# A two-layer transformer kernel whose written-out order of steps (an order table of letters) is replaced by another one

## What is computed

```python
x = x + L0_attn(layernorm(x))   # 16 heads of 8, causal softmax over 1024 tokens, W_qkv, W_out
x = x + L0_ffn(layernorm(x))    # ifft(fft(x) @ w), a real 128x128 matrix here, + bias
x = x + L1_attn(layernorm(x))   # the same attention, per-head 8x8 Wq, Wk, Wv, then Wu, bu
x = x + L1_ffn(layernorm(x))    # 8 experts of 256, the best 2 of a softmax gate, gelu
```

## Time and profile before

| | before |
|---|---|
| median of 3 runs (lowest to highest) | 1220.77 us (1218.82 to 1221.8) |
| the profiled execution: time / span of its trace | 1220.89 / 1219.2 us |
| busy in the span: TensorE, VectorE, ScalarE, GpSimd | 1132.4, 901.7, 770.1, 401.4 us |
| first shift copied at / last shift copied at | 78.9 / 923.4 us |
| last exponential of the last group ends | 958.4 us |
| the experts' steady chain begins | 986.9 us |

### The profile page before, as it was taken

One profiled execution on the slowest core, in us unless ns is written; L12 is line 12 of the kernel. 1 busy time (PEld: TensorE's weight loads), 2 busy tenths in 40 slices (PEclk: granted clock), 3 DMA queues, 4 the chain that ended last, 5 costly groups with the idle time before them and its releaser, 6 DMA issues. The chain is left out here.

```text
span 1219.2 us, 26837 instructions
## 1 busy us (share of the span) xinstructions
PE 1132.4 (93%) x9927; PEld 542.5 (44%) x9927; DVE 901.7 (74%) x1461; ACT 770.1 (63%) x1397; POOL 401.4 (33%) x667
## 2 busy tenths in 40 slices
PE   3479999999999999999999999999999799999997
PEld 2224343444344344433444344433342357777776
DVE  4698889998998999898899998898892253223223
ACT  1327678777888778787777787777777542322322
POOL 3143452555226462555356452142252000000000
PEclk9669999999999999899999999999998989999999
DMA  3230420112111011002111210011100000000000
GB/s 108 94 115 28 123 79 29 28 28 73 53 29 35 28 54 53 28 29 66 53 37 34 79 29 28 27 34 47 30 3 2 1 1 1 17 0 17 0 18 18
DMA packets 35336, 47.35 MB, mean 39 GB/s; under 512 B 8848, under 2 KB 15120, under 8 KB 35216
## 3 DMA queue, kind: packets, MB, share of 16 engines
...
q10 hardware_dynamic: 576, 0.15, 0.1%
...
## 5 line engine op out<-in xcount | busy, mean ns | idle before, releaser
L748 ACT ACTIVATE probs<-psum 128x512 f32<-128x512 f32 x1152 | 614.3, 604 | 199.8 <-PE psum L634 197.6
L930 DVE TENSOR_REDUCE block_max<-psum 128x8 f32<-128x1024 f32 x576 | 672.3, 1218 | 70.4 <-PE psum L602 67.0
L634 PE MATMUL psum<-q_rows,k_rows 50*128 50x512 bf16 (+3 forms) x1536 | 325.1, 330 | 14.4 <-ACT probs L748 10.9
L657 PE MATMUL psum<-probs,vg 128*32 128x512 f32 (+3 forms) x3072 | 329.0, 504 | 7.4 <-POOL probs L857 4.4
L857 POOL TENSOR_SCALAR_AFFINE_SELECT probs<-probs 128x512 f32<-128x512 f32 (+1 forms) x320 | 173.9, 547 | 448.0 <-ACT probs L748 444.4
L602 PE MATMUL psum<-k_rows,q_rows 48*128 48x128 bf16 (+2 forms) x2560 | 261.4, 266 | 27.8 <-DMA k_rows<-k_split 17.7
L602 PEld LDWEIGHTS psum<-k_rows,q_rows 48*128 48x128 bf16 x2560 | 114.7, 95 | 180.6 <-DVE block_max L930 74.9
L634 PEld LDWEIGHTS psum<-q_rows,k_rows 50*128 50x128 bf16 x1536 | 105.1, 94 | 166.0 <-ACT probs L748 124.0
L1162 DVE SCALAR_TENSOR_TENSOR x<-psum,probs,x 128x128 f32 x256 | 69.1, 343 | 144.4 <-PE psum L1080 144.0
L1102 ACT ACTIVATE probs<-psum 128x1024 f32<-128x1024 f32 x64 | 65.5, 1024 | 151.5 <-PE psum L1067 151.5
L1080 PEld LDWEIGHTS psum<-w_out,probs 128*128 128x128 f32 x1024 | 119.2, 192 | 14.8 <-issue 12.9
(11 more groups left out here) (107 smaller groups left out, 617.4 us busy)
## 6 DMA issues: line engine op xcount, KB each, us to landing
k_rows<-k_split SPq DMA_DIRECT2D x384, 32.0 KB
...
q_rows<-shift_t SPq DMA_DIRECT2D x64, 8.0 KB
```

The costliest lines, as they stand in the source:

```text
L634: done = nc.tensor.matmul(m.psum[:, bank, col:col + w], m.k_rows[rows_of(e, True), buf, pair, kb * P:(kb + 1) * P], m.q_rows[rows_of(e, Tr ...
L657: done = nc.tensor.matmul(m.psum[32 * hh:32 * hh + 32, OUT_BANK, q0 % BANK:q0 % BANK + w], m.vg[:, n % 2, kb, hh, :], m.probs[:, (n * len( ...
L748: nc.scalar.activation(out, m.psum[rows, UNIT_AT[number % UNIT_DEPTH], 0:columns], function, **more).then_inc(bank_read, 1)
L930: nc.vector.tensor_reduce(out, blocks, axis=AX.X, op=ALU.max).then_inc(ring_read, 1)
```

## The change

31 of the 33 lines of `LINES` are written anew, all but the first and the last; nothing else is touched. Every stream keeps its steps and their order, so the same instructions run, on the same engines, with the same sizes and numbers of buffers. The banks of the ring are given out in the new order. Two of the lines:

```diff
@@ -112,37 +112,37 @@
 LINES = (
     "xxxxxxxxxxxxxxxxxxxxwwwxxxxxxrrxxxrxxrxxrxxrxxrxxxxxxxrrrrrrrrrrrrrHrrr",
...
-    "uuvuruvruuvcruuurvOuruuvruxuruvuruvcxHuuvruruvuruuuvruruuuvruruuurvuruuwr",
...
-    "uxuvruvuruxruvcruuurvuOuruuvruuvruuuvcuuuvHuvuuuvuuuuvuuuuvuuu",
...
+    "uvruvuruuruvcruuxOuruuvruuruvvuruuvcruuruvruuvruruuvuruuxxuuuvuuHruvuuwrvvrxvc",
...
+    "uvruvuruuvcruuruvOuruuruvuvruuruvcuruuvruruuvuruuvruruuuvuuuuHvuuu",
     "uuvuvuuvcuuuvOuuuvvuuuvcuuuvuuuuvuuuuvuuuuvuuuuvuuuxxvvvcOxxxxxxxxxxxxxxxxxxx",
 )
```

More of the change, by code:

```diff
@@ L120 @@
[L120 to L137, removed]
@@ L145 @@
-    "uxuvruvuruxruvcruuurvuOuruuvruuvruuuvcuuuvHuvuuuvuuuuvuuuuvuuu",
+    "uuuruxxxxuruuruvuuuvvuuuvcuuuvuuxuvururuxuvruruxruuvruuxrurxuuvururuwxrxvxHvvxrrcxxO",
+    "uurxrxuuruuruvxxururuuuruvuvxrurxuuvcuruuxxxxxvuvuuurruvuuuuvuuuxuvuuruwxrxrxrvxxHvxxrrvxxcxr",
+    "uurxOxuruuruuvxxruruuuruuvrxuvxuruurvcuuruxvruuvruruuvruuuruvuHuuurruvuruw",
+    "uvruvuruuvcruuruvOuruuruvuvruuruvcuruuvruruuvuruuvruruuuvururuuvHuuuwrrvvrvc",
+    "uruuruuOuuruvruruuvuvruurxvcruuxrvuruuruuvruruuuvuruxxuuuvuuHruvuuuwrvrvx",
@@ new lines @@
+    "uruuvcruuruOuuruvxruruuvvuruuruvcxxruuvruruxxuvruruuuvruuxxuuuvuuHruvuuuwrvrvx",
+    "uruuvcruuruOuuruvrxuruuvuruvruuxxruvcruuurvruuvruuxxruruuvuruxHuuvruruxruuvrxuw",
+    "uxrxuruvuuvruruuvcruxxOuruxrxuurvuruxxrxxuurvvurxuurxuvcuruuvxuHuvruruuvuruuvruuruvuwr",
+    "uuvruuruvuruuvcruuruvOuruuvvruuxruvcruxruruuvuruuvHuuvruruuvuruuruvuruuwr",
+    "uuvruuruvuruuvcruuruvOuruuvvruuuvcruruuvruruuvuruuvHuuuvruruuuruvuruw",
+    "uvruvuruuruvcruuuOuruvuruuvruvruuuvcruruuvruruuvruuxxuuuvuHuurvuuuvruwrvvx",
@@ new lines @@
+    "uruuvcruuuruOuruuvrurxuuvurvuruuxvcrxruuvruuxxruvruruuvruuxxuuuvuuHruvuuuwrvrvx",
+    "uruuvcruuruOuuruvrxuruuvuruvruuxxruvcruuurvruuvruuxxruruuvuruxHuuvruruxruuvrxuw",
+    "uxrxuruvuuvruruuvcruxxOuruxrxuurvuruxxrxxuurvvurxuurxuvcuruuvxuHuvruruxuvruruxuvruruuvuwr",
+    "uruuvurvuruuvcruuruvOuruuvvruuuvcruruuvruuxxuuuvuHuruvuuuvruruuvuruuwr",
+    "uuvruvxuruuruvcruuuOuruvurxuurvuvruuuvcxrxruuvruruuvruuxxruvuHuuvruruuvuruuwr",
+    "uuvruvuruuruvcruuuOuruvuruurvuvruuuvcruruuvruruuvruuxxuuuvuuHvuruuvrxuwvrv",
@@ new lines @@
+    "uruuruuruuvcruuurvuOxuruuvruvxuruxruvcruuurvuruxxruuvruruuvuruxHuuvruruuvuwr",
+    "uxruurvuvurxuuruvcruuOuurxxruuvruurxxvruuvruuvcruxxruruuvuruxxxxxxHxvruruxuvruruxuvruruuvuwr",
+    "uruuvurvuruuvcruuruvOuruuvvruuuvcruruuvruuxxuuuvuHuruvuuuvruuruvuruuwr",
+    "uuvruvxuruuruvcruuuOuruvurxuurvuvruuuvcxrxruuvruruuvruuxxruvuHuuvruruuvuruuwr",
+    "uuvruvuruuruvcruuuOuruvuruurvuvruuuvcruruuvruruuvruuxxuuuvuuHvuruuvrxuwvrv",
+    "uruuruuruuvcruuurvuOxuruuvruvxuruxruvcruuurvuruxxruuvruruuvuruxHuuvruruuvuwr",
@@ new lines @@
+    "uxruurvuvurxuuruvcruuOuurxxruuvruurxxvruuvruuvcruxxruruuvuruxxxxxxHxvruruxuvruruxuvruruuvuwr",
+    "uruuvurvuruuvcruuruvOuruuvvruuuvcruruuvruuxxuuuvuHuruvuuuvruuruvuruuwr",
+    "uuvruvxuruuruvcruuuOuruvurxuurvuvruuuvcxrxruuvruruuvruuxruvuHuuvruruuvuruxruw",
+    "uvruvuruuruvcruuxOuruuvruuruvvuruuvcruuruvruuvruruuvuruuxxuuuvuuHruvuuwrvvrxvc",
+    "uuruOuururuuuvrxuruuvuruvruuxxruvcruuurvruuvruuxruruuvuruuvHuuurruvuruw",
+    "uvruvuruuvcruuruvOuruuruvuvruurxvcruuxrvuruuruvururuuvuruuxxuuuvuuHruvuuwrvvrxvc",
```

12 lines of the change are left out of this document (1 added, 11 removed).

## The result

| | before | after |
|---|---|---|
| median (lowest to highest), us | 1219.8 (1217.97 to 1221.8, 4 runs) | 1206.8 (1204.89 to 1209.52, 4 runs) |
| ratio, 95% interval | | 0.9898 [0.9882, 0.9913] |
| profiled execution / its span | 1220.89 / 1219.2 | 1209.52 / 1207.8 |

The account below looks back on a forecast made before the run. Neither engine alone was taken as bound: VectorE 90% full, TensorE nearly as full, time lost where long TensorE steps precede needed scores. 1220.9 - 6.2 (end) - 11.6 (places) + 2.1 + 1.8 = 1207.0 us; range 1193 to 1223, forecast's own 1200 to 1214.

Parts of the forecast that it names:

- The end: Behind the last shift: 3 units and one values step instead of 15 and 4 before group 31's first unit, 6.2 us less.
- The places: First to last shift: fewer scores, out steps and shifts right behind values steps, so VectorE idles 11.6 us less.
- +2.1: Ahead of the last shift: 12 units and 3 values steps moved there cost TensorE 0 to 4.2 us; middle taken.
- +1.8: Seven more shifts closely followed by their own group, waiting for the shift's DMAs: 0 to 3.6 us, middle taken.
- the dear place: Score directly behind a unit and a values step: its maximum found VectorE idle 0.248 us, against 0.037 at other scores.
- Norm steps: GpSimd's norm halves closer to their transpositions, ten first halves at the tight distance: 0 to 4 us, taken as 0.
- 1 (only the end): Nothing won in the middle, VectorE's idle time only moves; the end's gain stays: 1215 to 1219 us, chance 0.19.
- 6 (VectorE alone): VectorE the only bound, an order could close all its holes: 1128 us, chance 0.01.
- Of 2: More goes: the middle gives 22 us, nothing given back, perhaps one clock dip gone: 1193 us; below 1200, chance 0.11.
- the dip near 500 us: Granted clock at half around 500 us, VectorE idling 2.4 of 10 us instead of 1.0; it may go.
- Of 4: Slower through more stretches at half clock, about 1.4 us of VectorE each, some twelve more needed; chance 0.03.

Follow-up runs that it names:

- experiment 5: Kernel before with only the end of the order made as in the changed kernel (3 units and one values step behind the last shift): 1218.21 us, ratio 0.9990.
- experiment 3: Kernel before with 139 places 'unit, values, score' written as 'values, unit, score': 1228.29 us, ratio to before 1.0074.
- experiment 11: Kernel before with 36 values steps of the second half moved to later places only, by at most six letters: 1221.75 us, ratio 1.0011.
- experiment 6: Kernel before for its first 1229 letters (to about the shift of group 15), the changed kernel's order behind: 1201.65 us, ratio 0.9856.
- experiments 7 and 12: Each maximum taken over half of its columns only, in the changed kernel (7) and the kernel before (12): 1195.67 us (one run) and 1202.66 us.
- experiment 1: Changed kernel with its first 315 letters (up to the fourth shift) taken from the kernel before: 1201.4 us, ratio to before 0.9847.

## Why the prediction came out right, and where its reasons did not

The median, 1206.8 us, lies on the forecast of 1207.0; the profiled execution, on whose terms the sum was made, is 2.5 us over it. By its terms:

- **The end (-6.2).** Right in the trace: 6.5 us less from the last shift copy to the last exponential, the first unit 2.63 us behind the copy (forecast 2.65), the first unit waiting for the DMAs. What it costs ahead was mis-sized: I booked 2.1 us, with 4.2 as the most, and in experiment 5 the last two groups took 9.2 us more, with TensorE busy 6.5 us longer in them: the moved steps cost their full time there, and waits besides. By itself, as made there, the end won nothing clear of noise (1.7 us). How much the new table, which moved other steps with it, pays for its end is not shown.
- **The places (-11.6) with +2.1 and +1.8.** Forecast -7.7 between the first and the last shift copy, measured -4.9. The step that failed is that the mean idle time of a place is a price that goes with its neighbours: experiment 3 turned 139 places and lost 8 us, experiment 11 took 24 scores away from the dear place (190 to 166) and won nothing. As I read these runs, VectorE's idle time is where TensorE's lateness is seen, not where it is made. By lines: reciprocals 11.8 (forecast 11), shift copies 0.7 of the 2.2 (forecast half), maxima 59.3 (forecast 55). The first sign that I had named for a wrong forecast, idle time ahead of the maxima that stays near 60 and moves behind other steps, is there. In all VectorE idles 80.3 us there (839.60 - 759.26), where I had 78 to 80; the last shift is copied at 919.8, not 916, and the experts' chain begins at 975.6, not 973.
- **What won instead.** The second half, 8.0 us in the profiles and 11.3 in experiment 6. Three things differ there, and no run takes them apart. The cast's collisions with GpSimd, 3.8 us of VectorE before, are gone. The time at half clock went from 10.2 us to 6.8, and to none in experiment 6; at 1.5 us for 3.4 that is an estimated 1.5 us of the 8.0 and 4.5 of the 11.3. Some 3 us are left for the order itself, if the collisions cost all of their 3.8. With a light VectorE (experiments 7 and 12) 2.4 of the 8.0 us are left; at the same clock, by the same estimate, some 4 of 6.5. So how much of it lies where scores and maxima meet stays open, and so do the letters that carry it. The two ways of moving values steps alone that I tried, ahead of a unit (3) or later (11), won nothing.
- **What lost.** The start, 4.5 us, which no term had. The trace has collisions there (3.3 us of VectorE) and 3.4 us at half clock behind one; that these are the whole loss was not tried.
- **Tight hand-overs (+1.8).** Waits for the shift's DMAs grew by 5.3 us (4.1 to 9.4) in five more waits, over the 3.6 that I had as the most. How much of it reaches the end was not tried; experiment 6, faster than both kernels, has as much (9.6 us in 15).
- **Norm steps (0).** Nothing in the trace speaks against it.
- **The rivals.** 1 (only the end) and 6 (VectorE alone) fell: the middle did win, though not by less idle time ahead of the maxima, on which rival 1 was right, and 273 us less of VectorE's work won 10. Of 2, the dip near 500 us did go, but not the 22 us; its length also changed without a change of order (experiment 5). Of 4, a sign that I had named for a wrong forecast is there: three places at half clock between the first and the last shift instead of two (the three stretches above; before, they lay near 496 and 574 us). At two of them the shift that follows comes 1.6 and 1.5 us later than in experiment 1, which has none. In all, the half clock lasts as long as before between these copies (10.2 us), so it moves time from one part to another and does not carry the difference between the two kernels.

So the sum held because the second half won more than I had for the whole first stretch, and the start, which I had not looked at by itself, took the excess back. That the median lies 0.2 us from the forecast is luck: of the large terms only the shorter end is confirmed, its price and the places' gain are not.
